# Four attention blocks in one program: the last norm and final addition moved from GpSimd to VectorE, ScalarE's table loaded first, and every step reordered

## The reference

```python
# block 0: attention 0 (causal, 16 heads) and 1 (on the context), then a small MLP
x1 = layernorm(x + mha(x, x, causal=True), ln1);  x2 = layernorm(x1 + mha(x1, ctx), ln2)
x = layernorm(x2 + relu(x2 @ fc1.T + b1) @ fc2.T + b2, ln3)
# block 1: attention 2 on the context, then a SiLU MLP of width 512
x = x + attn(layernorm(x) @ Wq.T, layernorm(ctx) @ Wkv.T) @ Wo.T + bo
x = x + silu(x @ W1.T + b1) @ W2.T + b2
# block 2: attention 3 (causal), attention 4 on the context, ReLU MLP of width 512, each on a layernorm
# block 3: three layers i = 0, 1, 2 (attentions 5, 6, 7; 4 heads), first keys and values from the context
out = attn(relu(q @ Wq + bq), relu(k @ Wk + bk), relu(v @ Wv + bv)) + q
enc = gamma * (out - mean) / (std + 1e-8) + beta          # std with ddof=1
enc = leaky_relu(enc @ Wff + bff, 0.2) + enc              # q, k, v of the next layer
```

## Time and profile before

| | us |
|---|---|
| median of 3 runs | 1123.93 (1123.82 to 1132.66) |
| profiled execution, its own time | 1126.91 |
| its span, first to last instruction | 1125.1 |
| PE busy | 1041.3 (93%) |
| DVE busy | 828.8 (74%) |
| ACT busy | 595.9 (53%) |
| POOL busy | 333.1 (30%) |
| mean granted clock of PE | 0.983 |

### The profile page before, as it was taken

The page is one execution under the profiler, slowest core; times in us unless marked ns, Lnnn a source line. Parts: engine busy times, 40 slices in busy tenths (PEclk is TensorE's granted clock), DMA queues, the critical chain, the costliest instruction groups (busy, mean ns, idle before and its releaser), DMA issues.

```text
span 1125.1 us, 37457 instructions
## 1 busy us (share of the span) xinstructions
PE 1041.3 (93%) x16315; PEld 762.7 (68%) x16350; DVE 828.8 (74%) x2316; ACT 595.9 (53%) x857; POOL 333.1 (30%) x417
## 2 busy tenths in 40 slices
PE   7969889989999999989999999989999999999985
PEld 4648666657777776767676777656767777767664
DVE  5787889876476644788777878999576675669885
ACT  4425445555666455544554455545666655374552
POOL 4021145510110203354460312453100110235547
PEclk9989899989999999999999999999999999999999
DMA  7000000000000000000000000000000000000001
...
DMA packets 13716, 13.54 MB, mean 12 GB/s; under 512 B 617, under 2 KB 13170, under 8 KB 13298
## 3 DMA queue, kind: packets, MB, share of 16 engines
...
...
## 4 chain that ended last, share of the span: by engine, by line
PE 22%; DVE 22%; POOL 5%; issue 2%; ACT 2%; POOLq 0%; ACTq 0%; DVEq 0%
DVE mx L1285 5%; PE pair L687 5%; PE pair L915 3%; PE pair L886 3%; DVE stats L1032 3%; PE pair L881 3%; PE pair L756 2%; PE pair L674 2%; DVE Y L1088 1%; DVE Y L1042 1%; DVE Y L1050 1%; DVE X L1165 1%; DVE mv L1035 1%; PE pair L789 1%; DVE rq L1083 1%
## 5 line engine op out<-in xcount | busy, mean ns | idle before, releaser
L965 ACT ACTIVATE PT<-pair 128x1024 f32<-128x1024 f32 x184 | 183.4, 1026 | 149.8 <-PE pair L886 130.9
L1285 DVE TENSOR_REDUCE mx<-pair 128x16 f32<-128x1024 f32 x184 | 218.9, 1215 | 39.9 <-PE pair L886 39.5
L915 PEld LDWEIGHTS pair<-V,PT 128*64 128x64 f32 x5888 | 183.4, 138 | 33.6 <-issue 20.5
L915 PE MATMUL pair<-V,PT 128*64 128x32 f32 (+2 forms) x5888 | 197.4, 224 | 4.8 <-DVE Y L1088 2.0
L886 PEld LDWEIGHTS pair<-KQ 32*128 32x128 f32 (+3 forms) x4416 | 170.6, 158 | 40.4 <-issue 5.9
L886 PE MATMUL pair<-KQ 32*128 32x128 f32 (+3 forms) x4416 | 181.2, 255 | 3.0 <-DVE mx L1285 1.5
L687 PE MATMUL pair<-xf,W_all 128*128 128x512 f32 x336 | 176.9, 624 | 3.0 <-ACT xf L931 1.6
L1312 POOL TENSOR_SCALAR ve<-mv 128x4 f32<-128x4 f32 x64 | 16.3, 255 | 537.7 <-DVE mv L1035 506.8
L931 ACT ACTIVATE KQ<-pair,c 128x512 f32<-128x512 f32 x160 | 100.0, 688 | 66.2 <-PE pair L687 66.0
L663 PE MATMUL pair<-warm 128*128 128x512 bf16 x294 | 105.1, 391 | 9.2 <-ACT xf L931 1.6
L931 ACT ACTIVATE xf<-pair 128x512 f32<-128x512 f32 x80 | 47.5, 597 | 87.6 <-PE pair L674 87.3
...
## 6 DMA issues: line engine op xcount, KB each, us to landing
...
Xin<-x SPq DMA_DIRECT2D x8, 256.0 KB, 3.3
C<-ctx SPq DMA_DIRECT2D x8, 256.0 KB, 4.0
out<-X SPq DMA_DIRECT2D x8, 256.0 KB, 2.7
...
```

Of the source, the lines that this page charges most:

```text
L915: mm = pe.matmul(outputs[s][r, at:at + n], p[:, u, b, side, :], V[:, first:first + n], start=True, stop=True)
L965: act.activation(PT[:, place, :], banks.of("B", a, s, v)[:], ACT.Exp, scale=float((D // (2 * PAIRS[a])) ** -0.5)).then_inc(*banks.drain((" ...
L1285: dve.tensor_reduce(dst, banks.of("A", a, s, v)[:].rearrange("p (u m t) -> p u m t", u=2, t=S), AX.X, ALU.max).then_inc(*banks.drain(("A", ...
```

## The change

Four things are changed.

1. In the last group, at attention 8, DVE does what POOL did: behind its four `n1` instructions it waits for POOL's rstd and makes X = Y * rstd + beta in four instructions, and behind `leaky` it adds Y to X. POOL keeps the rstd steps. PE's `x1` and SP's last transfers wait for DVE there.
2. ACT has a new first instruction, a copy of one column of `warm` to a new tile `spare`, which waits only for POOL's first memset. The table load stands in front of it.
3. All four lists of ORDER are written anew. They hold the same steps, but for the eight of POOL that went away. The skeleton is kept: attention 3 of stream 0 in group 1, for one, ends with PE's step 796 in both lists.
4. There are 269 fillings instead of 294. By attentions, group 0 from 0 to 8: 31, 27, 39, 17, 15, 16, 13, 15, 2 before and 35, 25, 32, 20, 13, 18, 12, 5, 2 now; group 1: 24, 25, 31, 7, 11, 3, 5, 6, 7 before and 8, 23, 30, 4, 10, 3, 6, 11, 12 now.

```diff
--- before.py
+++ after.py
@@ -50,264 +50,265 @@
 ORDER = {
     "PE": """
-        0.0.0 x@7+2; 0.0.1 x@6; 0.0.0 pq@7+1; 0.0.3 x@5+1; 0.0.0 pk@4+1; 0.0.1 pq@7+1; 0.0.0 pv@6; 0.0.2 x@4; 0.0.0
+        0.0.0 x@7+1; 0.0.1 x@6; 0.0.2 x@7; 0.0.0 pq@6+1; 0.0.1 pq@5; 0.0.0 pk@4+2; 0.0.1 pk@7; 0.0.3 x@6+1; 0.0.2
...
@@ -552,6 +553,7 @@
         PT = sb("PT", [P, NPT, 1024])
         expo = sb("expo", [P, 3, NT])
         warm = sb("warm", [P, 128], BF16)
+        spare = sb("spare", [P, 1])
 
         section = Section(known)
         banks = Banks(ctx, nc, section)
@@ -644,7 +646,7 @@
                         sp.dma_start(C[s][:], c_g[section.group, s]).then_inc(*c_in[s].mark(by=16))
                 for section.group in range(GROUPS):
                     for s in range(STREAMS):
-                        sp.wait_ge(*pool.at("enc", 8, s))
+                        sp.wait_ge(*(vec if section.group == GROUPS - 1 else pool).at("enc", 8, s))
                         sp.dma_start(o_g[section.group, s], X[s][:]).then_inc(*x_out[s].mark(by=16))
                 for s in range(STREAMS):
                     sp.wait_ge(*x_out[s].at())
@@ -725,7 +727,7 @@
                             pe.wait_ge(*pool.at("enc", a, s))
                         turn(X[s] if a else Xin[s], use)
                     elif name == "x1":
-                        pe.wait_ge(*pool.at("x1", a, s))
+                        pe.wait_ge(*(vec if a == 8 and section.group == GROUPS - 1 else pool).at("x1", a, s))
                         turn(X[s], use)
                     elif name == "q":
                         pe.wait_ge(*vec.at("q", a, s))
@@ -1022,6 +1024,9 @@
                         return spent.at(a, s, v, ago=ago)
                     return banks.ready("O", a, s, v // 2 if PAIRS[a] == 8 else 1, ago=ago)
 
+                section.group = 0
+                act.wait_ge(*pool.at("warm"))
+                act.activation(spare[:], warm[:, 0:1], ACT.Copy)
                 walk("ACT", step)
 
             @block.vector
@@ -1042,14 +1047,26 @@
                         dve.tensor_scalar(dst[:, j, :], src[:, j, :], mv[lane(tag)][:, j, 0:1], rstd[lane(tag)][:, j:j + 1],
                                           ALU.subtract, ALU.mult).then_inc(*vec.mark(*tag))
 
+                def final(a):
+
+                    return a == 8 and section.group == GROUPS - 1
+
                 def norm_affine(name, *tag):
 
-                    s = tag[-1]
+                    a, s = tag[1:]
+                    i = lane(tag)
                     dve.wait_ge(*vec.at("mv", *tag))
                     for j in range(NT):
-                        dve.scalar_tensor_tensor(out=Y[s][:, j, :], in0=X[s][:, j, :], scalar=mv[lane(tag)][:, j, 0:1],
+                        dve.scalar_tensor_tensor(out=Y[s][:, j, :], in0=X[s][:, j, :], scalar=mv[i][:, j, 0:1],
                                                  in1=rowb(name + "_g"), op0=ALU.subtract, op1=ALU.mult
                                                  ).then_inc(*vec.mark("scaled", *tag))
+                    if final(a):
+                        dve.wait_ge(*vec.at("scaled", *tag))
+                        dve.wait_ge(*pool.at("rstd", *tag))
+                        for j in range(NT):
+                            dve.scalar_tensor_tensor(out=X[s][:, j, :], in0=Y[s][:, j, :], scalar=rstd[i][:, j:j + 1],
+                                                     in1=rowb(name + "_b"), op0=ALU.mult, op1=ALU.add
+                                                     ).then_inc(*vec.mark(*tag))
 
                 def absent(sums, a, s):
 
@@ -1223,6 +1240,9 @@
                         y = Y[s].rearrange("p j c -> p (j c)")
                         dve.scalar_tensor_tensor(out=y, in0=banks.of(*use)[:, 0:TOK], scalar=1.0, in1=y, op0=ALU.mult,
                                                  op1=ALU.max).then_inc(*banks.drain(use, vec, "leaky", a, s))
+                        if final(a):
+                            dve.wait_ge(*vec.at("leaky", a, s))
+                            dve.tensor_tensor(X[s][:], X[s][:], Y[s][:], ALU.add).then_inc(*vec.mark("enc", a, s))
                     elif name[:4] == "silu":
 
                         c = int(name[4])
@@ -1349,7 +1369,8 @@
                     elif name == "kvstats":
                         deviation(False, "kv", a, s)
                     elif name == "n1":
-                        affine(f"n{a}" if a < 3 else f"e{a}", "x1", a, s)
+                        if not (a == 8 and section.group == GROUPS - 1):
+                            affine(f"n{a}" if a < 3 else f"e{a}", "x1", a, s)
                     elif name == "n3":
                         affine("n3", "n3", a, s)
                     elif name == "n3q" or (name == "addwo" and a > 3) or (name == "addff" and a == 3):
@@ -1362,8 +1383,9 @@
                         g_.wait_ge(*(banks.ready("x", 3, s) if a == 3 else vec.at("q", a, s)))
                         add_bias(name, a, s)
                     elif name == "leaky":
-                        g_.wait_ge(*vec.at("leaky", a, s))
-                        g_.tensor_tensor(X[s][:], X[s][:], Y[s][:], ALU.add).then_inc(*pool.mark("enc", a, s))
+                        if not (a == 8 and section.group == GROUPS - 1):
+                            g_.wait_ge(*vec.at("leaky", a, s))
+                            g_.tensor_tensor(X[s][:], X[s][:], Y[s][:], ALU.add).then_inc(*pool.mark("enc", a, s))
 
                 walk("POOL", step)
 
```

501 lines of the change are left out of this document (251 added, 250 removed).

## The result

| | before | after |
|---|---|---|
| median, us | 1125.52 (4 runs) | 1098.09 (4 runs, 1095.0 to 1098.79) |
| ratio, 95% interval | | 0.974 [0.969, 0.979] |
| profiled execution, span | 1125.1 | 1096.3 |
| PE busy, idle in the span | 1041.3, 83.8 | 1030.7, 65.6 |
| time at half clock ahead of the end | 34.2 in six stretches | 27.3 in four |

The account below looks back on a forecast made before the run. PE, busy 93% of the span, was taken as the bound, losing time to idleness, fillings and half clock. Terms -5.0 + 1.0 - 1.0 + 0 + 0 = -5.0 gave a median of 1119.0 us, range 1108 to 1130.

Parts of the forecast that it names:

- The rest of the lists: All swaps elsewhere in the lists: same work, only PE's idle time and half clock can differ; 0, ends -9 and +8.
- the order frees more than fillings: Rival: new lists avoid four of six half-clock stretches, up to 9 us, giving 1110; chance 0.25 with neighbours beyond 1%.
- The fillings, -5.0: Whole program: 25 fillings fewer at 0.2 us each save 5.0 us; 0 if they only stood in waits.
- The 26 cuts: Fillings cut in attention 7 of group 0 (15 to 5) and attention 0 of group 1 (24 to 8).
- the others nearly cancel: Claim that changes in filling numbers outside attention 7 of group 0 and attention 0 of group 1 nearly cancel.
- the slower rival: Too few fillings, mainly in attention 0 of group 1: waits lie bare, PE's clock falls, 1135; chance 0.11.
- The start, +1.0: Program start: table load hidden, but first projection waits behind third input's transposes; net +1.0 us, ends -1.3 and +3.
- Behind `split`, -1.0: Steps after `split`: DVE's O0 moved behind nm frees PE's `maxrow` 1.0 us sooner; -1.0, ends -1.8 and 0.
- The end, 0: Last norms and additions on DVE: shorter chain, but DVE waits for rstd ahead of mrow; 0, ends -2.9 and +0.8.
- The promise of 2.9 us: Program end: the edit taken alone shortens the last chain by 2.9 us, from POOL's steps going to DVE.

Follow-up runs that it names:

- the lists alone: The new lists with their 269 fillings on the code of the kernel before: 1098.25 us, ratio to before 0.976.
- the single-step experiment: Kernel before with PE's transposes `q` of 0.3.0 moved behind `v1` of 0.2.2 and `maxrow` of 0.2.3: 1121.19 us, ratio to before 0.997.
- the new end: Changed kernel with another order of group 1's last steps, `mrow` of 1.7.3 right behind `nm`: 1097.66 us, ratio to before 0.975.
- after plus 26: Changed kernel with 26 fillings put back in attention 7 of group 0 and attention 0 of group 1: 1099.67 us, ratio to before 0.976.
- the code alone: Changed code (DVE's last norms and additions, ACT's table loaded first) on the lists of the kernel before: 1133.79 us, ratio to before 1.007.

## Why the prediction was wrong

**The failed step is "The rest of the lists. ... I take 0, with -9 ... as ends".** The low end was made of the half clock alone. What was measured in its place: the new order with its banks is worth 18 us with the old counts of fillings, and 27 with the new counts. PE's idle time, 83.8 us by the same page, stood in the first paragraph and in no term, though it is the first thing that an order changes: 18.2 us of it went in the trace of after, 11.2 with the lists alone. Not all of the gain is idle time, either. With the old counts on the new order the same 294 fillings take 105.1 us as before, idle time is 9.0 us less, and busy time 11.7 less, of which the half clock explains at most 4.8 (18.2 us of work at half clock, where before has 27.8). Why the rest of the same work is busy for less time wasn't followed; busy time is a union of overlapping matmuls. Even all the low ends together (-5.0 - 1.3 - 1.8 - 2.9 - 9 = -20.0) give 1103.9, 5.8 us above what was measured. The sentence "here I have no row for any one swap" was wrong too. The swap of one step in front of `B0` of 0.2.3 had its row, 1.50 us behind DVE's Y, with the half clock right behind it, and the one step moved gave 1.2 us of wait, and 3.0 more in an execution whose clock fell there. The list of PE's waits for DVE, taken through the program beside the two lists, was there to be read; I had looked at three places, and they brought a loss at the start, 1.7 us behind `split` and a loss of 0.9 at the end, none of the three stretches that gain.

**The rival "the order frees more than fillings" named the right cause and the wrong mechanism.** It expected the gain from stretches at half clock, 9 us. By the busy time in them, the stretches changed by 13.9 - 12.3 = 1.6 us in the profiled runs. Nor does the clock fall only "where PE starves for some microseconds". The first stretch of before, which was said to follow the idle time behind `split`, began 0.4 us into the wait of 3.96, behind waits of 1.03 and 0.79. At 246.28 the clock fell behind a wait of 1.50, at 601.27 behind one of 0.23, and in after it fell at 93.4 with PE busy in 19.88 us of the 20 from 80 to 100. What it said against itself, "the skeleton is kept", was no argument: at the single-step experiment the skeleton is kept but for one step. The prediction's last line had the true case among what would make it wrong, "many waits of under a microsecond, spread over the whole program", and gave it no chance of its own: PE's idle pieces of under a microsecond, from 20 us on, add up to 51.6 us before and 35.4 after.

**The fillings, -5.0.** No one number holds: the new counts cost some 4 us on the old order and are worth some 9 on the new one, and that -5.0 lies between is an accident. The 26 cuts were worth 0.8 us on the old order by the traces and nothing by the median, so there the end "0" of the term was right, and 1.6 by the medians on the new. But "the others nearly cancel" was wrong: their number cancels, their places don't, and these are worth some 7 us on the new order. Of the slower rival, bare waits and a falling clock, the first half holds where order and counts don't fit: with the new counts on the old order idle time is 91.7 us, 7.9 more, while the time at half clock ahead of the end is 34 us, as in before.

**The start, +1.0.** Mechanism right, size at its high end: the end of `split` comes 3.1 us later and 0.0.3 stands at +3.0. In two other traces with the same start, the new end and after plus 26, `split` ends 2.6 and 2.5 us later, and 0.0.3 stands at -0.3 and +0.4; their stretch at half clock behind `split` is 6.8 us long, after's 13.65. The transposes of the third input stood at 10.11 and not 9.2, and PE, idle for longer, did the projections behind them slowly (3.62 us for two). The other side of the term, 1.28 us for the table load, is 0: with the load moved and the old lists the first projection began 0.05 us sooner.

**Behind `split`, -1.0.** From the end of `split` to the end of nm it was 8.1 us before (60.71 to 68.84) and is 6.4 now (63.78 to 70.17), so the step is right by itself, with 1.7 in place of 1.0. But the end of `split` comes 3.1 us later, the half-clock stretch is 3.4 longer, and 0.0.2 stands at +0.9: what was gained paid for the start.

**The end, 0.** The chain of the working said +0.8, and 0.9 was measured, with the wait for rstd ahead of mrow as it had it. The promise of 2.9 us is not kept; the code alone loses 6.2 us between 1.4.2 and the end (+0.6 to +6.8), so the order around it wins most of that back. On the new lists DVE's norms are the better ones by the traces, 1.2 to 1.8 us lost behind 1.7.2 in the four with this end, against 2.0 to 4.3 with POOL's, though the medians (1098.09 and 1098.25) don't show it. Where the working said that "DVE works in order, and the new four wait for rstd", the code alone shows the waits: 1.97, 0.48, 1.97 and 1.00.

**Left open.** Why a cut between two orders costs some 4 to 6 us at one point and nothing at another was not followed through the lists; nor were the parts of the order and of the fillings in the 4.6 us at the change of groups told apart. How much of the order's 18 us is its other banks no run shows; the step moved by itself, banks unchanged, is the one place where the order alone was measured.
